# Two-input VectorE operations and two norms written as scalar-tensor-tensor operations

## The reference, cut to what matters

```
x, ctx: [32, 128, 512] float32                      # 32 batches, 128 tokens, 512 channels
x = x + wkv(w, u, k=layernorm(x), v=ctx)            # a scan over tokens: exp weights, ratio of two sums
x = x + attention(layernorm(x), Wa, Wp, ...)        # 16 heads, causal softmax, 8 dims of each head rescaled
x = x + mlstm(q=layernorm(x), k=ctx, v=ctx, ...)    # gates, running max, decayed scores, head norm
x = x + moe(layernorm(x), gate_w, w_gate, w_up, w_down)   # 32 experts, top 8, capacity, silu(g) * u
layernorm(x) = (x - mean) / sqrt(var + 1e-5)
```

## Time and profile before

| | |
|---|---|
| time, median of 3 | 2238.33 us (2236.39 to 2238.59) |
| the profiled execution | 2235.58 us, its span 2233.8 us |
| busy: TensorE, VectorE, ScalarE, POOL | 2041.8, 1682.9, 1149.9, 1541.2 us |
| first stage, steps 5 to 31 | one step each 32.11 us or a little more, from about 180 to 1037 us of the span |
| first stage, start and tail | 0 to 180 us and 1037 to about 1140 us |
| second stage (experts) | about 1140 us to the end |

### The profile page before, as it was taken

One profiled execution on the slowest core, in us unless ns is written; L12 is line 12 of the kernel. 1 busy time (PEld: TensorE's weight loads), 2 busy tenths in 40 slices (PEclk: granted clock), 3 DMA queues, 4 the chain that ended last, 5 costly groups with the idle time before them and its releaser, 6 DMA issues. The chain is left out here.

```text
span 2233.8 us, 67151 instructions
## 1 busy us (share of the span) xinstructions
PE 2041.8 (91%) x22647; PEld 1497.9 (67%) x22712; DVE 1682.9 (75%) x3294; ACT 1149.9 (51%) x2826; POOL 1541.2 (69%) x1776
## 2 busy tenths in 40 slices
PE   1899999999999999999509999999999999999997
PEld 1576667666666676666306777777777777777775
DVE  6688999999999999997426677676776677666664
ACT  3355555565555556555314455555555555555553
POOL 7336667666766666666667777777777777777774
PEclk9999999999999999999859999999999999999998
DMA  3101100110111001001016888887788878987875
GB/s 104 39 26 40 39 28 28 38 34 28 33 38 33 28 33 38 33 24 45 21 34 154 174 181 164 187 181 174 168 173 180 184 175 169 186 185 161 180 158 87
DMA packets 141452, 222.72 MB, mean 100 GB/s; under 512 B 32944, under 2 KB 65840, under 8 KB 141360
## 3 DMA queue, kind: packets, MB, share of 16 engines
q0 software_dynamic: 74752, 144.02, 32.8%
q1 hardware_dynamic: 62000, 69.24, 10.1%
q10 hardware_dynamic: 4608, 8.39, 1.0%
HBM read 136.34 MB, written 96.73 MB: 104 GB/s over the span
## 5 line engine op out<-in xcount | busy, mean ns | idle before, releaser
L2151 POOL DMA_INDIRECT out_dram<-y,m_add x300 | 499.1, 1664 | 173.8 <-POOLq L2159 116.8
L2277 PE MATMUL ps<-xh,wh 128*128 128x256 f16 x1752 | 399.9, 273 | 6.9 <-PEq L2289 6.9
L2278 PE MATMUL ps<-xh,wl 128*128 128x256 f16 x1752 | 399.9, 273 | 0.0
L2143 POOL DMA_INDIRECT xg<-z_scratch,slot_t x292 | 295.3, 1011 | 96.8 <-issue 86.2
L630 POOL DMA_INDIRECT slot_scratch<-pair,slots x256 | 277.5, 1084 | 68.8 <-issue 47.6
L2354 ACT ACTIVATE y<-ps,wts_now 128x512 f32<-128x512 f32 x294 | 185.4, 682 | 141.3 <-ACTq L2353 141.2
L2282 PE MATMUL ps<-xl,wh 128*128 128x256 f16 x1752 | 239.6, 273 | 0.0
L2428 DVE SCALAR_TENSOR_TENSOR hx<-ps,s 64x256 f16<-64x256 f32 x146 | 62.2, 426 | 219.3 <-DVEq L2451 218.6
L2277 PEld LDWEIGHTS ps<-xh,wh 128*128 128x128 f16 x1752 | 171.7, 98 | 48.7 <-issue 15.4
L2370 ACT ACTIVATE xh<-ps 128x512 f16<-128x512 f32 x146 | 87.2, 597 | 224.4 <-ACTq L2369 224.4
L2278 PEld LDWEIGHTS ps<-xh,wl 128*128 128x128 f16 x1752 | 171.8, 98 | 33.7 <-issue 0.3
(11 more groups left out here) (341 smaller groups left out, 5108.9 us busy)
## 6 DMA issues: line engine op xcount, KB each, us to landing
wst<-in_L_ffn_w_gate_dram SPq DMA_DIRECT2D x32, 384.0 KB
wst<-in_L_ffn_w_up_dram SPq DMA_DIRECT2D x32, 384.0 KB
xt<-in_x_dram SPq DMA_DIRECT2D x32, 256.0 KB
ct<-in_ctx_dram SPq DMA_DIRECT2D x32, 256.0 KB, 2.6
out_dram<-x SPq DMA_DIRECT2D x32, 256.0 KB, 2.1
z_scratch<-zn ACTq DMA_DIRECT2D x32, 256.0 KB
wdst<-in_L_ffn_w_down_dram SPq DMA_DIRECT2D x32, 256.0 KB
out_dram<-y,m_add POOLq DMA_INDIRECT x300, 5.2
```

Source lines behind the costliest of these rows:

```text
L2143: pool.indirect_dma_start(out=xg[b][:, h, :], out_offset=None, in_=z_d[:, :], in_offset=bass.IndirectOffsetOnAxis(ap=rows(h), axis=0)).the ...
L2151: pool.indirect_dma_start(out=acc_d[:, :], out_offset=bass.IndirectOffsetOnAxis(ap=m_add[:, k, h:h + 1], axis=0), in_=y[:, k, h, :], in_of ...
L2277: pe.matmul(ps[:, dst, 0:GROUP], wh[:, j, k, c0:c0 + P], xh[:, k, :], start=(k == 0), stop=False)
L2278: pe.matmul(ps[:, dst, 0:GROUP], wl[:, j, k, c0:c0 + P], xh[:, k, :], start=False, stop=False)
```

## The change

Six operations that combine two SBUF tiles elementwise (`tensor_tensor`) are written as `scalar_tensor_tensor` with a first operation that multiplies by 1.0: `(a * 1.0) op b`. Two of the four layernorms, `key_norm` and `query_norm`, are written as `scalar_tensor_tensor` too: `(x - mean) * rstd`, where `rstd`, one number per partition, is read as a tile of 512 columns by a broadcast of step 0; before, it was a second per-partition scalar of a `tensor_scalar`. The other two norms (`xn` at L1659, `zn` at L1782) stay as they are. The operands, the results, the waits and the order of all instructions on all engines are the same; only the form of these eight VectorE instructions differs, in each of the 32 batches.

```
-                    return dve.tensor_tensor(ol[:, :, :], oT[:, :, :], oh[:, :, :], ALU.subtract)
+                    return dve.scalar_tensor_tensor(flat(ol), flat(oT), 1.0, flat(oh), ALU.mult, ALU.subtract)
...
-                    return dve.tensor_scalar(kn[:, :], xt[:, :], mv[0][:, 0:1], rstd[0][:, 0:1], ALU.subtract, ALU.mult)
+                    return dve.scalar_tensor_tensor(kn[:, :], xt[:, :], mv[0][:, 0:1], rstd[0][:, :].to_broadcast([P, D]), ALU.subtract, ALU.mult)
...
-                    return dve.tensor_tensor(gv[:, :, :], gg[:, :, :], vT[:, :, :], ALU.mult)
+                    return dve.scalar_tensor_tensor(flat(gv), flat(gg), 1.0, flat(vT), ALU.mult, ALU.mult)
...
-                    return dve.tensor_scalar(qn[:, :], x2[:, :], mv[2][:, 0:1], rstd[2][:, 0:1], ALU.subtract, ALU.mult)
+                    return dve.scalar_tensor_tensor(qn[:, :], x2[:, :], mv[2][:, 0:1], rstd[2][:, :].to_broadcast([P, D]), ALU.subtract, ALU.mult)
...
-                    return dve.tensor_tensor(cv[:, :, :], cc[:, :, :], vT[:, :, :], ALU.mult)
+                    return dve.scalar_tensor_tensor(flat(cv), flat(cc), 1.0, flat(vT), ALU.mult, ALU.mult)
...
-                    return dve.tensor_tensor(cv[:, :, 1:T], cv[:, :, 1:T], sp_[:, :, 0:T - 1], ALU.add)
+                    return dve.scalar_tensor_tensor(cv[:, :, 1:T], cv[:, :, 1:T], 1.0, sp_[:, :, 0:T - 1], ALU.mult, ALU.add)
...
-                    return dve.tensor_tensor(gv[:, :, :], cc[:, :, :], rden[:, :, :], ALU.mult)
+                    return dve.scalar_tensor_tensor(flat(gv), flat(cc), 1.0, flat(rden), ALU.mult, ALU.mult)
...
-                    return dve.tensor_tensor(fm[:, :], cum[:, :], cmx[:, :], ALU.add)
+                    return dve.scalar_tensor_tensor(fm[:, :], cum[:, :], 1.0, cmx[:, :], ALU.mult, ALU.add)
```

## The result

The changed kernel takes 2243.27 us (median of 8 executions, 2240.07 to 2246.43); the kernel before, run beside it, takes 2236.2 us (8 executions, 2234.03 to 2238.59). The ratio is 1.0032 with a 95% interval of 1.0021 to 1.0043: 7.1 us slower, by the interval 4.7 to 9.6. The forecast was 4.4 us slower. One execution of the kernel before, beside the last experiment, took 3906.85 us at a granted clock of 0.81 and is left out there.

The account below looks back on a forecast made before the run. No engine by itself bounds the kernel; a chain through TensorE's wait for `qn` does. 4.4 us for `qn` and 0 for the rest, added to the 2238.33 us median, gave 2242.7 us, range 2238.0 to 2250.0.

Parts of the forecast that it names:

- Which engine and which place: At the query norm `qn`, TensorE's wait for it ends last, so all engines take over its delay in full, once per step.
- The count of 30: Instructions of `query_norm` on the path: 27 full steps, two before them and the last in the tail; 4.4 us in all.
- The price of a norm: Each rewritten norm on VectorE goes from 534 to 681 ns, 147 ns longer (126 to 158).
- The key norm at nothing: The longer `key_norm` costs 0, covered by VectorE's wait for `xnh`; without that cover, another 4.0 us.
- The six tensor-tensor operations at nothing: Both forms cost the same and wait for POOL alike: cost 0, -0.6 to +0.2 us in all.
- How the steps can fall: Order in which POOL's L688 and VectorE's L1655 reach SBUF, or `hw` meets L1742, may change: -3.3 to +5 us.
- Hidden: Rival at TensorE's wait for `qn`: something else ends as late, so the 0.15 us vanish; 2238.3 us, chance 0.08.
- Scalar-tensor-tensor does not wait for POOL: Rival: `gv` and `fm` end 1.12 and 0.85 us earlier, step some 0.5 us shorter; 2224.8 us, chance 0.06.
- `denominator_error` falls onto `scale_heads`: Rival: VectorE's L1742 meets POOL's `hw` more often, 1.19 us per step, perhaps in 8 steps; 2252 us, chance 0.10.
- Half rate: Rival: the new form runs at half rate, `qn` and `gv` together 1.25 us longer per step; 2272 us, chance 0.02.

## Why the prediction was right, and where its size was off

**Which engine and which place.** Right. The wait that ends last is TensorE's for `qn`; the distance of 0.30 us from its end to the turn stayed while `qn` grew, and the line L1713 alone gives the ratio of the whole change (1.0032 both).

**The count of 30.** Right, as far as it can be read: 26 full steps grew by 5.13 us (0.197 each), and the last `qn` came 6.08 us later, against 29 x 0.205 = 5.95.

**The price of a norm.** This term was mis-sized, and it is the step of the prediction that failed. The forecast took 681 ns, with 660 and 692 as ends, from scalar-tensor-tensor rows whose scalar is a constant; the prediction itself said that no row had the form with a per-partition scalar, and then let the nearest rows stand as ends. The form takes 739 ns, outside these ends. What was missing is the fixed 62 ns of the per-partition scalar. Nothing in the trace excluded such a cost, so the upper end should not have been put at the slowest row of another form. Two rows of the kernel before even pointed to it, tensor-scalar operations of 128 columns, the first with two per-partition scalars and the second with a constant:

```profile
L1757 DVE TENSOR_SCALAR nx<-cmx,nmul,nadd x32: 345/346/348, 103.9 to 1094.0; 128x128 f32<-128x128 f32 x32
L1638 DVE TENSOR_SCALAR fm<-fm x32: 192/196/533, 112.7 to 1103.2; 128x128 f32<-128x128 f32 x32
```

The 150 ns between them are about twice 62, with one operation more in the first. With 0.205 instead of 0.147 us the sum is 30 x 0.205 = 6.2 us, and the measured 7.1 (4.7 to 9.6) holds it. The old 4.4 lies just outside. That the forecast time, 2242.7 us, is only 0.6 us from the measured 2243.27 is luck: it started from a median of three executions, 2238.33 us, which was 2.1 us above the later one of eight, and this nearly made up for a difference that was 2.7 us too small.

**The key norm at nothing.** Right. The wait for `xnh` took up the longer norm, as the prediction said (6.0 us of it before, 0.2 with the key norm alone), and its time, 1.0009 (1.0000 to 1.0017), leaves at most a small rest, which the larger delay ahead of the key norm (1.0001) doesn't confirm. Behind it stands a second cover that the prediction didn't see: VectorE takes TensorE's projection 0.15 us after its end, with and without a delay ahead of it.

**The six tensor-tensor operations at nothing.** Right: ratio 1.0001, same durations, same wait for POOL, same 0.55 us to the release.

**How the steps can fall.** This term was put at -3.3 to +5 us and came out at nothing: 26 steps grew by 5.13 us where 26 x 0.205 is 5.33. That it can come to something is shown by the operation ahead of the query norm, with 3.0 us. The prediction read it partly wrong: L1655 takes 0.40 us only in the steps of 32.25, while in those of 32.42 it takes 0.87.

**The rivals.** *Hidden* fell: the step went from 32.11 to 32.32. *Scalar-tensor-tensor does not wait for POOL* fell: `gv` still takes 1.79 us. *`denominator_error` falls onto `scale_heads`* fell: L1742 takes 0.68 us in the step shown, and its median is 0.68 too. *Half rate* fell by the prices above: the rate is that of tensor-tensor, and `cv` and `gv` didn't grow.

**What was not foreseen.** The prediction said that a delay of `qn` is passed on in full and is silent on the other direction. In the runs the two differ: a later `qn` cost its whole delay in both sizes tried (0.2 and 0.33 us), and the one move that made it earlier at no other cost gained nothing that could be told from none (0.9994, 0.9984 to 1.0004), since POOL's DMA got longer and its product at L663 held VectorE.

## What to carry to other kernels

Rewriting a tensor-scalar operation on float32 SBUF tiles as scalar-tensor-tensor doubles its price per column (0.51 to 1.04 ns here), so the loss grows with the columns; a per-partition scalar comes on top as a fixed charge. Here a rewrite of tensor-tensor with a constant 1.0 was free and brought nothing. Where a form is missing from a trace, look at which of its parts no row has (here the per-partition scalar) and leave room above the slowest neighbour, instead of taking that neighbour as the bound. Before an operation is moved off the wait that ends last, look for the next place at which another engine's work sets the date; if that date is tied to something else, a delay can be paid in full while an advance is not paid out.

## What the runs showed of the hardware that I had not expected

- A tensor-scalar operation of float32 SBUF tiles costs 0.51 ns for each column (534 ns at 512, 404 at 256), scalar-tensor-tensor and tensor-tensor 1.04 (684 and 419).
- The per-partition scalar of a scalar-tensor-tensor operation costs a fixed 62 ns (746 against 684 ns at 512 columns, 480 against 419 at 256), and an innermost broadcast of step 0 as the second tile costs nothing (686 against 684).
- A VectorE operation with two SBUF inputs can be held by POOL's indirect DMA and then by the product behind it: the scan of the kernel with the query norm first was issued at 511.85, 0.56 us before `cc`, and took 2.93 us. The Trainium skill, "SBUF — State Buffer", section "Who interferes with whom", has a single exclusive lock on the shared ports, and by its section "SBUF: two separate sides" the one that starts first keeps it for its whole length. The traces agree only in part. Counted from the products alone, the scan came first and should have ended after 1.27 us, so the DMA takes part in the lock. But it doesn't hold for its whole length: in the kernel before, L1742 was issued 0.14 us after the DMA's start (516.90 and 516.76), and both took their unheld time, 0.68 and 1.01 us; the scan L1745, issued 0.74 us after that start, took 1.86 us instead of 0.42.
- The hold goes the other way, too: the same indirect DMA takes 1.01 us before and 1.46 us where a VectorE operation of two SBUF inputs (L1742, 0.68 us) was issued 0.11 us ahead of it (516.20 and 516.31).
- A tensor-scalar operation that is held is let go sooner than one with two SBUF inputs: `qn` ends 0.30 us behind `cc` (507.50 + 1.53 = 509.03, `cc` 507.45 + 1.28 = 508.73), `gv` 0.55.
